# Adjacency as byte pairs in a two-layer graph attention kernel, with VectorE emptying the transposed banks and ScalarE comparing 104 of 128 units

## Chip, cores and metric

One core of a Trainium2 chip runs the whole program. The metric is the device time of one execution in microseconds (us); lower is better.

## What is computed

`x` is 4096 x 128 (f32), `adj` is 4096 x 4096 (int32, 0 or 1, about 1 in 500 is set, the diagonal always). Two layers of masked attention follow each other, each with a residual and a layer norm:

```python
# layer 0, four heads of 32
Wh = (h @ W).reshape(N, H, D)
e = s_src[:, None, :] + s_dst[None, :, :]
e = jnp.where(e >= 0, e, 0.2 * e)
e = jnp.where(adj[:, :, None] > 0, e, NEG_INF)
h_prime = einsum('ijh,jhd->ihd', softmax(e, axis=1), Wh);  elu
# layer 1, one head of 128, the same mask
x_tan = _logmap0(x);  e = leaky_relu(x_tan @ a[:D] + (x_tan @ a[D:]).T, 0.2)
x_tan_prime = softmax(where(adj > 0, e, NEG_INF), axis=1) @ x_tan
return _proj(_expmap0(x_tan_prime))
```

The exponential of a leaky sum splits into factors of i and of j on either side of zero. So for each pair (i, j) the kernel needs only two bits: is j a neighbour, and is s_i + d_j negative. The softmax becomes two mask products, one with the mask of all neighbours (or of those above zero) and one with the mask of those below, times weighted values held as three bf16 parts.

## The kernel before

**Chunks and units.** The first layer goes over 4 chunks (`NC`) of 1024 rows i. In a chunk there are 32 units `u`: head `h` (4) times group `g` of `JU` = 4 tiles of 128 columns j. A unit has a slot in `ring` (4 slots), each with two halves of 128 x 4096 bytes, "above" and "below".

**What a unit costs each engine.** Either ScalarE (`act_unit`, L741) or VectorE (`dve_compare`, L756) compares: four instructions of 128 x 1024, one per tile j, each reading f32 and writing one byte. The string "AVAVAAVA", repeated, says who: 20 units of 32 on ScalarE, 12 on VectorE. VectorE then ANDs the result with the masks (L777 after ScalarE, L781 after itself). For a unit that is not `DIRECT` it also XORs to get "above" (L786). `DIRECT` is "DD-D----" repeated, 12 of 32. TensorE (`pe_chunk`, L825) does 8 row tiles times 4 tiles j, two matmuls each: two of 99 columns for a unit that is not direct; one of 99 with `masks` and one of 198 with "below" for a direct one. Each loads 128 x 128 fp8 weights, a contiguous 128 bytes per partition.

**Masks.** GpSimd issues casting DMAs (`load_adj`, L399) that bring 128 rows of `adj` into one of two bf16 tiles. TensorE transposes 8 blocks of 128 x 128 at a time (`turn_group`, L413) into one of four banks. ScalarE empties the bank into `raw_masks` (`take_group`, L421). There are 32 such groups in a chunk (`QT` = 4 per tile). In the end VectorE turns `raw_masks` into `masks` with 8 instructions (`clean_masks`, L493). `masks` is one buffer. The groups for chunk c + 1 are turned between units 6 and 27 of chunk c; ScalarE takes them 3 units later. SyncE stores `masks` to DRAM for the second layer (`keep`, L854) and reloads rows of scores.

**Order.** Each engine runs its units in order. A compare of unit u waits until TensorE is done with unit u - 4. After the last unit of a head, VectorE reduces four banks (L795) and weighs them (L210 to L223), which frees the banks for TensorE. The steps that close a chunk (L688 to L714) lie between the first units of the next. Chunks 0 to 2 are in a loop with register counts.

**Start.** `x` is loaded in four parts; then tile 0 and tile 1 of the adjacency are loaded, and tile t once the tile t - 1 is turned and the queue comes to it. Between the 16 steps of the projection (L565), from step 8 on, TensorE turns one group per step, 8 in all. VectorE then finds bounds (L149 to L171), and prepares weighted values (`prepare_sides`, L460 to L469) with casts on ScalarE (`round_sides`, L481), between which ScalarE takes three groups at a time. Then VectorE cleans all masks of chunk 0 and the block of units starts (first compare at 91.65 us). GpSimd weighs one of the sides (L436) after its eight tile loads.

**Second layer.** 8 runs of 512 rows; `load_masks` (L1008) fetches the masks, ScalarE (L1250) and VectorE (L1350) compare half of the tiles each (512 elements), TensorE multiplies 387 columns at a time (L1283, the first run L1301).

```python
    ON_ACT = [who == "A" for who in H * "AVAVAAVA"]
    DIRECT = [how == "D" for how in H * "DD-D----"]
            act.activation(dst[:, j:j + GQ, t * P:(t + 1) * P],
                           turn_bank[q % 4][:, :].bitcast(BF16).rearrange("p (j i) -> p j i", i=P),
                           ACT.Relu, scale=2.0, saturate=False).then_inc(turned_out, 1)
            dve.tensor_scalar(masks[:, :].bitcast(I32)[:, here], raw_masks[:, :].bitcast(I32)[:, here], TWOS, SIGNS,
                              ALU.bitwise_and, ALU.bitwise_or).then_inc(mask_ready, 1)
```

Of the kernel before, what the change touches and what calls it, by code (L numbers as in the profile page):

```python
# [15 lines left out]
F32, BF16, FP8, I32, U8 = (mybir.dt.float32, mybir.dt.bfloat16, mybir.dt.float8e4, mybir.dt.int32, mybir.dt.uint8)  # L16
# [4 lines left out]
P = 128  # L21
# [8 lines left out]
TWOS = 0x40404040  # L30
SIGNS = 0x80808080 - (1 << 32)
# [21 lines left out]
def two_layer_gat(nc, x, adj, W, a0, a1, out):  # L53
# [3 lines left out]
    x_rows = x.rearrange("(t p) f -> p t f", p=P)  # L57
    out_rows = out.rearrange("(t p) f -> p t f", p=P)
# [12 lines left out]
    ON_ACT = [who == "A" for who in H * "AVAVAAVA"]  # L71
# [13 lines left out]
    LAG = 3  # L85
# [16 lines left out]
    masks_kept = nc.dram_tensor("masks_kept", (NC, P, T, C // 4), I32, kind="Internal").ap()  # L102

    ctx = ExitStack()
    with ctx:
# [120 lines left out]
        def general_attention(layer, heads, width, flag_ap, d_rows_dram, s_of, values_in, summed, finish):  # L226
# [3 lines left out]
            with local:  # L230
# [13 lines left out]
                B = N // BANK  # L244
                with nc.Block() as block:
                    @block.sync
                    def _(sp):
                        with sp.If(sp.value_load(flag_ap, min_val=0, max_val=1) > 0):
                            sp.dma_start(d_rows[:, :, :], d_rows_dram.rearrange("(o h) n -> o h n", o=1)
                                         .broadcast_to([P, heads, N])).then_inc(loaded, 16)  # L250
                            if values_in is None:
                                sp.dma_start(v[:, :, :], values_kept).then_inc(loaded, 16)
                            with sp.Fori(0, T) as it:
                                sp.wait_ge(adj_used, it + 1)
                                sp.dma_start(adj_tile[:, :], adj[bass.ds(it * P, P), :]).then_inc(adj_in, 16)

                    @block.vector
                    def _(dve):
                        with dve.If(dve.value_load(flag_ap, min_val=0, max_val=1) > 0):
                            dve.memset(rowwise[:, 3:4], 0.0).then_inc(adj_used, 1)  # L260
                            dve.wait_ge(loaded, 16 if values_in is not None else 32)
                            with dve.Fori(0, T) as it:
                                dve.wait_ge(adj_in, it * 16 + 16)
                                dve.tensor_scalar(keep[:, :], adj_tile[:, :], 0.0, None, ALU.is_gt).then_inc(chain, 1)
                                dve.tensor_scalar(away[:, :], adj_tile[:, :], 0.0, -NEG_INF, ALU.is_le, ALU.mult)\
                                    .then_inc(adj_used, 1)
                                for h in range(heads):
                                    q = it * heads + h
                                    c = it * (5 * heads + 1) + 5 * h + 1
                                    dve.wait_ge(chain, c)  # L270
                                    dve.tensor_scalar(e[:, :], d_rows[:, h, :], s_of(it, h), None, ALU.add).then_inc(chain, 1)
                                    dve.wait_ge(chain, c + 1)
                                    dve.scalar_tensor_tensor(out=e[:, :], in0=e[:, :], scalar=SLOPE, in1=e[:, :],
                                                             op0=ALU.mult, op1=ALU.max).then_inc(chain, 1)
                                    dve.wait_ge(chain, c + 2)
                                    dve.tensor_tensor(e[:, :], e[:, :], keep[:, :], ALU.mult).then_inc(chain, 1)
                                    dve.wait_ge(chain, c + 3)
                                    dve.wait_ge(adj_used, it + 2)
                                    dve.tensor_tensor(e[:, :], e[:, :], away[:, :], ALU.add).then_inc(chain, 1)
                                    dve.wait_ge(chain, c + 4)  # L280
                                    dve.reduce_max(rowwise[:, 0:1], e[:, :], axis=AXX).then_inc(chain, 1)
                                    dve.wait_ge(chain, c + 5)
                                    dve.tensor_scalar(rowwise[:, 1:2], rowwise[:, 0:1], -1.0, None, ALU.mult)\
                                        .then_inc(masked, 1)
                                    dve.wait_ge(expd, q + 1)
                                    dve.reciprocal(rowwise[:, 3:4], rowwise[:, 2:3]).then_inc(normed, 1)
                                    for n in range(B):
                                        dve.wait_ge(turned, q * B + (n + 1))
                                        dve.tensor_copy(eT[:, n % 2, :], bank[n % 2][:, :]).then_inc(turned_out, 1)
                                    dve.wait_ge(sums, q + 1)  # L290
                                    dve.wait_ge(normed, q + 1)
                                    dve.tensor_scalar(one(summed[:, bass.ds(it, 1), h * width:(h + 1) * width]),
                                                      bank[2][:, 0:width], rowwise[:, 3:4], None, ALU.mult)\
                                        .then_inc(given, 1)
# [64 lines left out]
        idle = masks[:, :].bitcast(F32)  # L359
# [26 lines left out]
        adj_in = sems("adj_in0", "adj_in1")  # L386
        a1_taken, turned, turned_out, mask_ready, kept, pool_done = sems(
            "a1_taken", "turned", "turned_out", "mask_ready", "kept", "pool_done")
# [8 lines left out]
        def load_adj(pool, b, t):  # L397

            pool.dma_start(adj_tiles[:, t % 2, :], adj[bass.ds(b * C + t * P, P), :]).then_inc(adj_in[t % 2], 16)  # L399

        def turn_group(pe, b, q):

            t = q // QT
            if q % QT == 0:
                pe.wait_ge(adj_in[t % 2], b * (8 * CT) + 16 * (t // 2 + 1))
            if isinstance(b, int) and b == 0 and q < 4:
                pass
            else:
                hold(pe, turned_out, b * Q + (q - 3))
            dst = turn_bank[q % 4][:, :].bitcast(BF16)  # L410
            for k in range(GQ):
                j = (q % QT) * GQ + k
                last = pe.transpose(dst[:, k * P:(k + 1) * P], adj_tiles[:, t % 2, j * P:(j + 1) * P], ident_b[:, :])  # L413
            last.then_inc(turned, 1)

        def take_group(act, b, q):

            t, j = q // QT, (q % QT) * GQ
            hold(act, turned, b * Q + (q + 1))
            dst = raw_masks[:, :].rearrange("p (j i) -> p j i", i=C)  # L420
            act.activation(dst[:, j:j + GQ, t * P:(t + 1) * P],  # L421
                           turn_bank[q % 4][:, :].bitcast(BF16).rearrange("p (j i) -> p j i", i=P),
                           ACT.Relu, scale=2.0, saturate=False).then_inc(turned_out, 1)
# [64 lines left out]
        def clean_masks(dve, b, g):  # L488

            if g == 0:  # L490
                dve.wait_ge(turned_out, b * Q + Q)
            here = slice(g * (JU * C // 4), (g + 1) * (JU * C // 4))
            dve.tensor_scalar(masks[:, :].bitcast(I32)[:, here], raw_masks[:, :].bitcast(I32)[:, here], TWOS, SIGNS,  # L493
                              ALU.bitwise_and, ALU.bitwise_or).then_inc(mask_ready, 1)

        with nc.Block() as block:
            @block.sync
            def _(sp):
# [3 lines left out]
                for k in range(XPARTS):  # L502
                    some = slice(k * T // XPARTS, (k + 1) * T // XPARTS)
                    sp.dma_start(feat[:, some, :], x_rows[:, some, :]).then_inc(x_in[k], 16)
# [13 lines left out]
            def _(pool):  # L518
# [98 lines left out]
            def _(dve):  # L617
# [46 lines left out]
                for g in range(UH):  # L664
                    clean_masks(dve, 0, g)

# [52 lines left out]

        def act_count(u):  # L720
# [9 lines left out]
        def act_unit(act, c, u):  # L730
# [18 lines left out]
        def dve_compare(dve, c, u):  # L749
# [10 lines left out]
        def dve_unit(dve, c, u, clean=False):  # L760
# [4 lines left out]
            if clean and g + 1 < UH:  # L765
                clean_masks(dve, c, g + 1)
# [3 lines left out]
            m = masks[:, :].bitcast(I32)[:, g * (JU * C // 4):(g + 1) * (JU * C // 4)]  # L770
            done = unit_ready if DIRECT[u] else below_ready
            if clean:
                dve.wait_ge(mask_ready, c * UH + (g + 1))
# [28 lines left out]
        def pe_chunk(pe, c, build):  # L802

            for u in range(U):
# [6 lines left out]
                for t in range(CT):  # L811
# [3 lines left out]
                    for k in range(JU):  # L815
                        j = g * JU + k
                        mine = slice(k * C + t * P, k * C + (t + 1) * P)
                        if DIRECT[u]:
                            of_all = masks[:, j * C + t * P:j * C + (t + 1) * P]
                            weighed = ((of_all, 0, PARTS * K0), (below[:, mine], 0, W0))  # L820
# [613 lines left out]
```

## Time and profile before

| | us |
|---|---|
| three executions | 1074.44, 1074.69, 1074.98 (median 1074.69) |
| the profiled execution, first to last instruction (span) | 1073.5 |
| start, to the first compare of chunk 0 | 91.65 |
| chunk 0, then 1, 2, 3, each to the first bank reduced of its last head | 134.9, 138.0, 137.5, 128.0 |
| from there to the end | 443.5 |
| busy: TensorE, VectorE, ScalarE, GpSimd | 901.4, 897.8, 608.6, 51.3 |

The page gives the profiled execution's span and no separate time of its own; the span is 1.2 us under the median of the three. Busy times of TensorE include modelled ends, so a matmul's price is read from the distance between starts and not from its duration. On VectorE successive instructions overlap a little, so there too start to start is used where it matters.

### The profile page before, as it was taken

The numbers are of one execution on the slowest core, as the hardware profiler recorded it, in microseconds if no ns is written. First come the engines' busy times: TensorE is split into PE (matmuls) and PEld (weight loads), VectorE is DVE, ScalarE is ACT, GpSimd is POOL, SyncE is SP. The second block draws the span as 40 slices with busy tenths as digits, with TensorE's granted clock in tenths as the row PEclk, the third lists the DMA queues.
The fourth block names the chain that finished last, engine by engine and source line by source line (L and its number), as shares of the span: only waits on it lengthen the run. The fifth ranks groups of instructions, "written<-read, shape, count | busy, mean of one in ns | idle before, by whom it ended". The sixth has DMA issues, their size and how long they took to land. (4 is left out here: it accounts for less than half of the span.)

```text
span 1073.5 us, 27634 instructions
## 1 busy us (share of the span) xinstructions
PE 901.4 (84%) x11508; PEld 744.5 (69%) x11508; DVE 897.8 (84%) x1648; ACT 608.6 (57%) x672; POOL 51.3 (5%) x59
## 2 busy tenths in 40 slices
PE   7644999987999889998888950388999999999990
PEld 6534999987999889998787950354555555555550
DVE  6956888989998999988999976989888788778825
ACT  3685899967899677996755711344414225134101
POOL 1030000000000000000000000800000000000000
PEclk9756999989999999999999985689999999999996
DMA  8865355615555245530210003301130321303000
GB/s 179 221 118 190 82 116 108 108 35 184 104 109 104 59 159 118 99 82 22 126 54 22 2 1 101 79 1 50 49 89 12 99 60 39 89 16 92 0 10 11
DMA packets 50686, 85.88 MB, mean 80 GB/s; under 512 B 1346, under 2 KB 42756, under 8 KB 45828
## 3 DMA queue, kind: packets, MB, share of 16 engines
q0 software_dynamic: 4608, 33.56, 17.1%
q1 hardware_dynamic: 41732, 48.47, 14.3%
q10 hardware_dynamic: 4224, 2.10, 0.7%
q8 instruction: 92, 1.51, 0.6%
q14 instruction: 30, 0.25, 0.1%
HBM read 96.54 MB, written 21.14 MB: 110 GB/s over the span
## 5 line engine op out<-in xcount | busy, mean ns | idle before, releaser
L825 PE MATMUL bank<-moving,ring 128*128 128x99 bf16 (+1 forms) x6656 | 455.7, 219 | 18.9 <-DVE ring L786 18.9
L825 PEld LDWEIGHTS bank<-moving,ring 128*128 128x128 fp8e4 x6656 | 390.9, 98 | 24.3 <-issue 11.5
L741 ACT ACTIVATE ring<-s_rows,scores 128x1024 fp8e4<-128x1024 f32 x320 | 340.5, 1141 | 107.9 <-PE bank L825 97.6
L1283 PE MATMUL bank<-moving,pair 128*128 128x387 bf16 x1792 | 299.9, 329 | 3.8 <-DVE evac L1372 3.8
L1283 PEld LDWEIGHTS bank<-moving,pair 128*128 128x128 fp8e4 x1792 | 175.6, 98 | 128.1 <-DVE evac L1372 4.2
L825 PE MATMUL bank<-moving,masks 128*128 128x99 bf16 x1536 | 211.8, 211 | 33.3 <-DVE evac L795 18.0
L825 PEld LDWEIGHTS bank<-moving,masks 128*128 128x128 fp8e4 x1536 | 152.5, 100 | 33.4 <-issue 24.7
L756 DVE TENSOR_SCALAR ring<-s_rows,neg_d 128x1024 uint8<-128x1024 f32 x192 | 131.5, 748 | 10.4 <-PE bank L825 6.6
L1210 ACT ACTIVATE small<-small 128x4 f32<-128x4 f32 x24 | 4.9, 205 | 219.1 <-DVE small L1156 180.3
L421 ACT ACTIVATE raw_masks<-bank 128x1024 fp8e4<-128x1024 bf16 x128 | 121.9, 1028 | 6.8 <-PE bank L413 5.2
L777 DVE SCALAR_TENSOR_TENSOR ring<-ring,masks 128x1024 int32<-128x1024 int32 x80 | 97.6, 1220 | 20.9 <-ACT ring L741 20.9
L413 PE MATMUL bank<-ident_b,adj_tiles 128*128 128x128 bf16 x1024 | 78.9, 232 | 26.7 <-ACT raw_masks L421 16.0
L786 DVE TENSOR_TENSOR ring<-masks,ring 128x1024 int32<-128x1024 int32 x80 | 98.0, 1225 | 2.7
L1250 ACT ACTIVATE pair<-s_rows,scores 128x512 fp8e4<-128x512 f32 x128 | 79.5, 708 | 20.7 <-DVE result L1190 16.2
L413 PEld LDWEIGHTS bank<-ident_b,adj_tiles 128*128 128x128 bf16 x1024 | 67.3, 104 | 31.3 <-ACT raw_masks L421 12.6
L1372 DVE TENSOR_REDUCE evac<-bank 128x129 f32<-128x387 f32 x64 | 31.6, 553 | 43.3 <-PE bank L1283 37.2
L1350 DVE TENSOR_SCALAR pair<-s_rows,neg_d 128x512 uint8<-128x512 f32 x128 | 58.6, 521 | 0.0
L781 DVE TENSOR_TENSOR ring<-ring,masks 128x1024 int32<-128x1024 int32 x48 | 58.5, 1218 | 0.0
L1301 PE MATMUL bank<-moving,pair 128*128 128x387 bf16 x256 | 44.3, 336 | 15.7 <-DVE pair L1362 15.7
L1301 PEld LDWEIGHTS bank<-moving,pair 128*128 128x128 fp8e4 x256 | 25.5, 100 | 34.4 <-issue 17.8
L1362 DVE TENSOR_TENSOR pair<-pair 128x1024 int32<-128x1024 int32 x32 | 39.2, 1225 | 1.1
L399 POOL DMA_DIRECT2D adj_tiles<-in_adj_dram x32 | 19.2, 601 | 433.9 <-PE bank L413 414.1
(218 smaller groups left out, 602.7 us busy)
## 6 DMA issues: line engine op xcount, KB each, us to landing
adj_tiles<-in_adj_dram POOLq DMA_DIRECT2D x32, 1024.0 KB, 8.4
masks_kept<-masks SPq DMA_DIRECT2D x4, 4096.0 KB, 13.0
pair<-masks_kept SPq DMA_DIRECT2D x8, 2048.0 KB, 9.8
s_rows<-score_rows SPq DMA_DIRECT2D x16, 512.0 KB, 3.6
feat<-in_x_dram SPq DMA_DIRECT2D x4, 512.0 KB, 6.1
values_kept<-masks SPq DMA_DIRECT2D x1, 2048.0 KB, 12.2
s_rows<-score_rows SPq DMA_DIRECT2D x8, 256.0 KB, 9.6
out_dram<-result ACTq DMA_DIRECT2D x8, 256.0 KB, 2.3
```

The source lines that it names most:

```text
L413: last = pe.transpose(dst[:, k * P:(k + 1) * P], adj_tiles[:, t % 2, j * P:(j + 1) * P], ident_b[:, :])
L421: act.activation(dst[:, j:j + GQ, t * P:(t + 1) * P], turn_bank[q % 4][:, :].bitcast(BF16).rearrange("p (j i) -> p j i", i=P), ACT.Relu, s ...
L741: last = act.activation(below[:, k * C:(k + 1) * C], s_rows[:, h % 2, :], ACT.Sign, bias=scores[:, j, h:h + 1], saturate=False)
L756: last = dve.tensor_scalar(below[:, k * C:(k + 1) * C], s_rows[:, h % 2, :], neg_d[:, h, j:j + 1], float(TWO), ALU.is_lt, ALU.mult)
L777: dve.scalar_tensor_tensor(out=below, in0=below, scalar=1, in1=m, op0=ALU.logical_shift_right, op1=ALU.bitwise_and).then_inc(done, 1)
L781: dve.tensor_tensor(below, below, m, ALU.bitwise_and).then_inc(done, 1)
L786: dve.tensor_tensor(above, m, below, ALU.bitwise_xor).then_inc(unit_ready, 1)
L825: last = pe.matmul(bank[b][:, at + lo:at + hi], mask, moving[:, j, h, lo:hi], start=first, stop=(j == T - 1), skip_group_check=True)
L1250: last = act.activation(pair[:, y, 1, j * R:(j + 1) * R], s_rows1[:, y, :], ACT.Sign, bias=scores1[:, j, 0:1], saturate=False)
L1283: last = pe.matmul(bank[2 * t + side][:, 0:PARTS * K1], pair[:, y, side, j * R + t * P:j * R + (t + 1) * P], moving1[:, j, side * PARTS * ...
L1301: last = pe.matmul(bank[2 * t + side][:, 0:PARTS * K1], pair[:, 0, side, j * R + t * P:j * R + (t + 1) * P], moving1[:, j, side * PARTS * ...
L1350: last = dve.tensor_scalar(below[:, j * R:(j + 1) * R].bitcast(U8), s, neg_d1[:, 0, j:j + 1], float(TWO), ALU.is_lt, ALU.mult)
```

## The change

Adjacency is cast to bytes and not to bf16, and two neighbouring bytes of a row are transposed as one bf16. So a tile has 16 transposes, not 32, and a chunk 16 groups (`QT` = 2), not 32. Rows and columns are numbered so that tile 2q + r holds the elements of parity r of 256. In `masks` and in both halves of a slot the bytes of tiles 2q and 2q + 1 alternate. Every compare therefore writes bytes at a step of 2, and every weight load of L825 and L1283 reads 128 bytes at a step of 2.

The bank is emptied by a multiply and an add on 16-bit integers straight into `masks`; `raw_masks` and `clean_masks` are gone, `masks` has two buffers, and `featT` and `values` lie in the second. In chunk 0 ScalarE still empties (16 groups); for chunks 1 to 3 VectorE does (16 each, after unit u it takes the groups of step u - 2). Four adjacency tiles are loaded ahead, not two. ScalarE compares 26 of 32 units, VectorE 6; 14 of 32 are direct. Loops over chunks are written out. The second layer's mask loads and the loads of `x` and stores of the result have runs twice as long.

```diff
-    ON_ACT = [who == "A" for who in H * "AVAVAAVA"]
+    ON_ACT = [who == "A" for who in H // 2 * ("AVAAAAVA" "AAVAAAAA")]
-    DIRECT = [how == "D" for how in H * "DD-D----"]
+    DIRECT = [how == "D" for how in H // 2 * ("DD-D----" "DD-D-D--")]
-    QT = T // GQ
+    QT = PAIRS // GQ
+    AHEAD = 4
-    LAG = 3
+    DVE_LAG = 2
-        masks = sb("masks", [P, T * C], FP8, fast0)
-        raw_masks = sb("raw_masks", [P, T * C], FP8, fast0)
+        masks = sb("masks", [P, 2, T * C], FP8, fast0)
-        adj_tiles = sb("adj_tiles", [P, 2, N], BF16, fast0)
+        adj_tiles = sb("adj_tiles", [P, AHEAD, N], U8, fast0)
-        idle = masks[:, :].bitcast(F32)
+        idle = masks[:, 1, :].bitcast(F32)
...
+        def take_group_dve(dve, b, q):
+            t, j = q // QT, (q % QT) * GQ
+            dve.wait_ge(turned, b * Q + (q + 1))
+            dst = masks[:, b % 2, :].bitcast(U16).rearrange("p (j i) -> p j i", i=C)
+            dve.tensor_scalar(dst[:, j:j + GQ, t * P:(t + 1) * P],
+                              turn_bank[q % 4][:, :].bitcast(U16).rearrange("p (j i) -> p j i", i=P),
+                              float(TWO), BOTH_SIGNS, ALU.mult, ALU.add).then_inc(turned_out, 1)
...
-                load_adj(pool, 0, 1)
-                for t in range(2, CT):
-                    pool.wait_ge(turned, (t - 1) * QT)
+                for t in range(1, AHEAD):
+                    load_adj(pool, 0, t)
+                for t in range(AHEAD, CT):
+                    pool.wait_ge(turned, (t - AHEAD + 1) * QT)
                     load_adj(pool, 0, t)
...
-                for g in range(UH):
-                    clean_masks(dve, 0, g)
...
+        def j_tile(half, k):
+            return half.rearrange("p (q i r) -> p q i r", i=C, r=2)[:, k // 2, :, k % 2]
-                last = act.activation(below[:, k * C:(k + 1) * C], s_rows[:, h % 2, :], ACT.Sign,
+                last = act.activation(j_tile(below, k), s_rows[:, h % 2, :], ACT.Sign,
...
-                last = dve.tensor_scalar(below[:, k * C:(k + 1) * C], s_rows[:, h % 2, :], neg_d[:, h, j:j + 1],
+                last = dve.tensor_scalar(j_tile(below, k), s_rows[:, h % 2, :], neg_d[:, h, j:j + 1],
...
+            if u == 0:
+                dve.wait_ge(turned_out, (c + 1) * Q)
...
                         for u in which:
-                            dve_unit(dve, c, u, clean)
+                            dve_unit(dve, c, u)
+                            if c + 1 < NC:
+                                for q in groups_at(u - DVE_LAG):
+                                    if q == 0 and c > 0:
+                                        dve.wait_ge(unit_done, SLOTS + c * U)
+                                        dve.wait_ge(kept, c * 16)
+                                    take_group_dve(dve, c + 1, q)
```

## Rows read from the trace of the kernel before

**Rows 1.** The page: busy time of each engine

```profile
PE 901.4 (84%) x11508; PEld 744.5 (69%) x11508; DVE 897.8 (84%) x1648; ACT 608.6 (57%) x672; POOL 51.3 (5%) x59
```

**Rows 2.** Busy time by chunk: window, length, PE, PEld, DVE, ACT, POOL, clock, DMA share

```profile
91.60:226.50 134.90, 125.51 (x2304) 124.58 (x2304) 115.58 (x146) 121.86 (x120) 6.18 (x10) 0.96 0.55 127
226.50:364.50 138.00, 126.24 (x2304) 124.22 (x2304) 128.69 (x182) 114.73 (x113) 5.07 (x8) 0.98 0.47 109
...
502.00:630.00 128.00, 112.21 (x2004) 110.06 (x2005) 121.47 (x173) 77.34 (x73) 0.00 (x0) 0.96 0.12 43
```

**Rows 3.** VectorE's groups in chunk 1: busy us, mean ns, idle before them

```profile
L756 DVE TENSOR_SCALAR ring<-s_rows,neg_d 128x1024 uint8<-128x1024 f32 x48 | 32.8, 747 | 2.1 <-PE bank L825 1.4 <-DVE attended L223 0.7
L786 DVE TENSOR_TENSOR ring<-masks,ring 128x1024 int32<-128x1024 int32 x20 | 24.5, 1225 | 0.7
L493 DVE TENSOR_SCALAR masks<-raw_masks 128x1024 int32<-128x1024 int32 x8 | 5.4, 686 | 0.1
```

**Rows 4.** Waits in chunk 1: us in total, times, longest

```profile
ACT ring L741 <- PE bank L825: 21.2, 8, 9.3
PE bank L825 <- DVE evac L795: 4.9, 2, 4.2
```

**Rows 5.** ScalarE's timeline: the four compares of a unit; eleven banks emptied

```profile
240.25 4.25 ACT L741 ACTIVATE ring<-s_rows,scores 128x1024 fp8e4<-128x1024 f32 x4
67.62 10.16 ACT L421 ACTIVATE raw_masks<-bank 128x1024 fp8e4<-128x1024 bf16 x11
```

**Rows 6.** TensorE's timeline at full clock: one group turned, one unit, direct pairs

```profile
324.80 0.61 PE L413 MATMUL bank<-ident_b,adj_tiles 128*128 128x128 bf16 x8
325.24 3.08 PE L825 MATMUL bank<-moving,ring 128*128 128x99 bf16 x64
333.11 0.25 PE L825 MATMUL bank<-moving,ring 128*128 128x198 bf16 x1
...
333.88 0.25 PE L825 MATMUL bank<-moving,ring 128*128 128x198 bf16 x1
```

**Rows 7.** Weight loads in chunk 1's lines: of fp8, and of bf16

```profile
L825 PEld LDWEIGHTS bank<-moving,ring 128*128 128x128 fp8e4 x1632 | 94.7, 97 | 6.6 <-issue 6.4
L413 PEld LDWEIGHTS bank<-ident_b,adj_tiles 128*128 128x128 bf16 x256 | 15.3, 97 | 1.8 <-issue 1.8
```

**Rows 8.** VectorE reading a bank: 128 and 396 elements

```profile
69.04 0.29 DVE L658 TENSOR_SCALAR mean_values<-bank 128x128 f32<-128x128 f32 x1
L795 DVE TENSOR_REDUCE evac<-bank 128x132 f32<-128x396 f32 x16 | 8.3, 561 | 0.5 <-PE bank L825 0.3
```

**Rows 9.** VectorE's and TensorE's timelines at the end of the start

```profile
85.17 4.91 DVE L493 TENSOR_SCALAR masks<-raw_masks 128x1024 int32<-128x1024 int32 x8 [15.58 <-ACT raw_masks L421]
91.65 2.79 DVE L756 TENSOR_SCALAR ring<-s_rows,neg_d 128x1024 uint8<-128x1024 f32 x4 [1.57 <-PEq L878]
97.54 0.24 PE L825 MATMUL bank<-moving,masks 128*128 128x99 bf16 x1 [14.06 <-DVE ring L777]
```

**Rows 10.** Timelines of GpSimd and TensorE in the start

```profile
10.06 0.72 POOL L399 DMA_DIRECT2D adj_tiles<-in_adj_dram  x1 [7.97 <-DMA feat<-in_x_dram]
11.75 0.53 POOL L399 DMA_DIRECT2D adj_tiles<-in_adj_dram  x1 [0.97 <-DMA feat<-in_x_dram]
72.38 1.92 POOL L436 TENSOR_TENSOR ring<-masks,below_d 128x1024 f32<-128x1024 f32 x1
26.33 0.61 PE L413 MATMUL bank<-ident_b,adj_tiles 128*128 128x128 bf16 x8
```

**Rows 11.** Landing of the loads issued at 10.06 and at 11.75 us

```profile
DMA to landing us min/median/max: 8.2/8.2/8.2
DMA to landing us min/median/max: 11.4/11.4/11.4
```

**Rows 12.** The chain of waits in the second layer: VectorE's compares, then TensorE

```profile
731.55 1.67 DVE pair L1350 x4
748.81 299.92 PE bank L1283 x1792
```

More of the change, by code:

```diff
@@ L56, in two_layer_gat, with paired, adj_rows @@
     T = N // P
-    x_rows = x.rearrange("(t p) f -> p t f", p=P)
-    out_rows = out.rearrange("(t p) f -> p t f", p=P)
+    PAIRS = N // (2 * P)
+    x_rows = x.rearrange("(q p r) f -> p q (r f)", p=P, r=2)
+    out_rows = out.rearrange("(q p r) f -> p q (r f)", p=P, r=2)
+    def paired(ap):
+        return ap.rearrange("p (q r) f -> p q (r f)", r=2)
+    def adj_rows(q, r):
+        some = bass.ds(q * 2 * P, 2 * P) if not isinstance(q, int) else slice(q * 2 * P, (q + 1) * 2 * P)
+        return adj[some, :].rearrange("(p r) n -> r p n", r=2)[r]
     CT = 8
@@ L252, in _ @@
                                 sp.dma_start(v[:, :, :], values_kept).then_inc(loaded, 16)
-                            with sp.Fori(0, T) as it:
-                                sp.wait_ge(adj_used, it + 1)
-                                sp.dma_start(adj_tile[:, :], adj[bass.ds(it * P, P), :]).then_inc(adj_in, 16)
+                            with sp.Fori(0, PAIRS) as iq:
+                                for r in range(2):
+                                    sp.wait_ge(adj_used, iq * 2 + (r + 1))
+                                    sp.dma_start(adj_tile[:, :], adj_rows(iq, r)).then_inc(adj_in, 16)
                     @block.vector
@@ L261, in _ @@
                             dve.wait_ge(loaded, 16 if values_in is not None else 32)
[L262 to L294, printed above, removed]
@@ L385, in two_layer_gat @@
             "mean_ready", "exp_asked", "exp_given", "scores_out", "values_out")
-        adj_in = sems("adj_in0", "adj_in1")
-        a1_taken, turned, turned_out, mask_ready, kept, pool_done = sems(
-            "a1_taken", "turned", "turned_out", "mask_ready", "kept", "pool_done")
+        adj_in = sems(*(f"adj_in{k}" for k in range(AHEAD)))
+        a1_taken, turned, turned_out, kept, pool_done = sems("a1_taken", "turned", "turned_out", "kept", "pool_done")
         s_in = sems("s_head_in0", "s_head_in1")
@@ L404, in turn_group @@
             if q % QT == 0:
[L405 to L409, printed above, removed]
+                pe.wait_ge(adj_in[t % AHEAD], 16 * (b * (CT // AHEAD) + t // AHEAD + 1))
+            if b > 0 or q >= 4:
+                pe.wait_ge(turned_out, b * Q + (q - 3))
             dst = turn_bank[q % 4][:, :].bitcast(BF16)
+            src = adj_tiles[:, t % AHEAD, :].bitcast(BF16)
             for k in range(GQ):
                 j = (q % QT) * GQ + k
-                last = pe.transpose(dst[:, k * P:(k + 1) * P], adj_tiles[:, t % 2, j * P:(j + 1) * P], ident_b[:, :])
+                last = pe.transpose(dst[:, k * P:(k + 1) * P], src[:, j * P:(j + 1) * P], ident_b[:, :])
             last.then_inc(turned, 1)
@@ L842, in _ @@
                 with only_if(pool, flag[0:1, 0:1], False):
-                    with pool.Fori(0, NC - 1) as c:
+                    for c in range(NC - 1):
                         for t in range(CT):
-                            pool.wait_ge(turned, c * Q + (Q + (t - 1) * QT))
+                            pool.wait_ge(turned, c * Q + (Q + (t - AHEAD + 1) * QT))
                             load_adj(pool, c + 1, t)
@@ L862, in load_s @@
                             .then_inc(s_in[h % 2], 16)
-                    with sp.Fori(0, NC - 1) as c:
+                    for c in range(NC - 1):
                         keep(c)
@@ L879, in _ @@
                     pe.sem_inc(acc_taken, NB)
-                    with pe.Fori(0, NC - 1) as c:
+                    for c in range(NC - 1):
                         pe_chunk(pe, c, True)
@@ L907, in _, with units @@
                 with only_if(dve, flag[0:1, 0:1], False):
-                    def units(c, which, clean=False):
+                    def units(c, which):
                         for u in which:
-                            dve_unit(dve, c, u, clean)
+                            dve_unit(dve, c, u)
[5 more added lines that the diff above has]
+                                    take_group_dve(dve, c + 1, q)
                             for h in range(H - 1):
@@ L918, in close @@
                         finish_ask(dve, attended[:, :, :], elu_asked)
-                    dve.wait_ge(mask_ready, UH)
                     units(0, range(DVE_ROT))
-                    with dve.Fori(0, NC - 1) as c:
+                    for c in range(NC - 1):
                         units(c, range(DVE_ROT, U))
-                        hold(dve, kept, c * 16 + 16)
-                        dve.wait_ge(unit_ready, c * U + U)
-                        clean_masks(dve, c + 1, 0)
                         for u in range(DVE_ROT):
-                            units(c + 1, (u,), u < UH)
+                            units(c + 1, (u,))
                             if u == CLOSE_AT:
@@ L1211, in close_act @@
             act.wait_ge(result_ready, e + 1)
-            act.dma_start(out_rows[:, run_rows(e), :], result[:, y, :, :]).then_inc(stored[y], 16)
+            pairs = bass.ds(e * (RT // 2), RT // 2) if not isinstance(e, int) else slice(e * RT // 2, (e + 1) * RT // 2)
+            act.dma_start(out_rows[:, pairs, :], paired(result[:, y, :, :])).then_inc(stored[y], 16)
         with nc.Block() as block:
```

123 lines of the change are left out of this document (76 added, 47 removed).

## The prediction, made before the change was run

> **What bounds the kernel now.** I read the page first. TensorE and VectorE are both busy for 84% of the span [rows 1], which settles nothing, so I cut the span into stages and asked in each which wait ends last.
>
> The start lasts 91.65 us. VectorE has finished its preparing at 69.6 us, stands idle for 15.58 us until ScalarE has emptied the last bank of turned adjacency, and then cleans all masks of chunk 0, 4.91 us; 1.6 us after that the units begin [rows 9]. So the emptying and the cleaning bound the start.
>
> In chunk 1 VectorE is busy 128.7 of 138.0 us, ScalarE 114.7 [rows 2]. Chunk 2 reads the same. TensorE's own need I work out from starts: a unit that isn't direct has 64 matmuls 45.7 ns apart, (3.08 - 0.21) / 63, so 2.92 us; a direct pair takes 128.3 ns, 0.77 us for six, so 4.11 us for the unit's 32; a transpose takes 56 ns, (0.61 - 0.216) / 7, the single durations being 0.21 and 0.216 us [rows 6]. 12 x 4.11 + 20 x 2.92 + 256 x 0.056 = 122.1 us. VectorE bounds chunks 1 to 3, with 9.3 us of gaps and waits in chunk 1. In chunk 0, without the closing steps, VectorE is busy only 115.6 us and TensorE is the heaviest with 122.1; the chunk takes 134.9. Of the 12.8 us above TensorE's need, 5.9 pass before its first matmul [rows 9] and about 3 are lost while its first unit runs at the lower clock. That leaves 4 us as the price of three nearly equal engines sharing four slots.
>
> In the second layer TensorE's matmuls run through for 299.9 us [rows 12]; nothing there is removed.
>
> **The change, part by part.**
>
> *Start.* 16 groups fewer for ScalarE are 16 x 0.92 = 15 us (10.16 us for eleven) [rows 5], and the cleaning goes. If nothing else were late, the units would begin at 69.6 + 1.6 = 71.2 us, 20.4 us sooner. But something is late next: the eight groups turned between the projection's steps now need tiles 0 to 3, where before they needed 0 and 1. Tile 0 lands at 10.06 + 8.2 = 18.3 us and tile 1 at 11.75 + 11.4 = 23.15, 4.9 us behind it in one queue [rows 10, 11]. At that pace tile 3 lands at 32.9 us, and the turn that waits for it stood at 26.33 us [rows 10]. Everything behind it in TensorE's order (the rest of the projection, then bounds and preparing) moves by 6.5 us. Units begin at 77.7: **-14**. The ends: -20.4 with no delay; if each tile took the whole 8.2 us, tile 3 lands at 42.9 and it is -4. GpSimd's weighing, at 72.4 us behind its eight issues [rows 10], follows tile 3's turn in place of tile 7's and comes sooner. The same holds for its later loads: their waits fall earlier.
>
> *VectorE in a chunk.* 24 compares go: 32.8 x 24/48 = 16.4 us. 8 cleans go: 5.4. Two XORs go: 2 x 1.22 = 2.5 [rows 3]. For six units the AND changes its form and not its price. What comes is 16 banks emptied, 128 x 1024 from a bank of 16-bit integers; no row has this. From below: the clean is the same operation on the same number of elements, 0.686 us [rows 3]. From above: bank reads of f32 take 0.29 us for 128 elements and 0.56 for 396 [rows 8], 1.01 ns an element, so 1.20 us. I take 0.67, as the clean is nearest in operation and size; +10.8 us, at most +19. Chunk 1's busy time becomes 128.7 - 24.3 + 10.8 = 115.2 us.
>
> The Trainium skill (VectorE: DVE Perf Modes, What auto-detection actually checks) says that two elements a cycle from a bank need every operand to be 16-bit at a step of 1, which holds here and not for the rows of f32. By its cycle table (120 + 512 cycles at 0.96 GHz) the estimate is 0.66 us, which would leave the sum as it is.
>
> *ScalarE.* 26 units x 4.27 = 111 us and 1 for the exponential, from 85.4 + 30 + 1 before [rows 5]: 112, unchanged in sum for chunks 1 and 2. The work is shifted from banks, which waited for nothing urgent, to compares, which TensorE waits for. The runs of six such units (25.6 us against 21 us of matmuls) have to be covered by its lead; it waited 21.2 us for slots in chunk 1 [rows 4], so there is some.
>
> *TensorE.* 14 x 4.11 + 18 x 2.92 + 128 x 0.056 = 117.3 us, 4.8 less; in chunk 3, without turns, 110.1, 2.3 more. Byte steps of 2 I take at nothing in all three engines: fp8 loads of 128 contiguous bytes and bf16 loads over 256 bytes both take 97 ns [rows 7], so the span of bytes isn't what a load costs.
>
> *New waits.* After unit u VectorE waits for the turn of step u - 2, with its next unit behind it, and TensorE behind that. TensorE does that turn before unit u - 2, and the next compare waits for unit u - 3 anyway; nothing. TensorE's turn needs the group four back, taken about three units ago; nothing. At unit 0 VectorE waits for groups it has emptied itself. SyncE's store of masks waits for the same count, with score rows behind it, and has more time than now. Written-out loops cost fetches of code beside a DMA share of 0.47 [rows 2]; nothing. In the second layer longer runs make loads shorter that are hidden.
>
> *Sum.* TensorE is now the heaviest, with VectorE at 115 and ScalarE at 112. Chunk 0: 117.3 plus the same 12.8, some 131: -4. Chunk 1: 117.3 plus 4 for sharing slots plus 4.9 for the banks of the last head, which it waits for now too [rows 4], 126.5: -11.5. Chunk 2: -11. Chunk 3: ScalarE 112 is the heaviest, VectorE 121.5 - 16.4 - 3.4 (five cleans) - 2.5 = 99; with 8 us of waits 120: -8. Together -14 - 4 - 11.5 - 11 - 8 = **-48.5 us** on a span of 1073.5, which stands 1.2 us under the median. Against the median it gives 1026 us.
>
> **Rivals.**
>
> *A, banks at one element a ns.* 8 us more on VectorE: 123 + 9.3 in chunks 1 and 2, so -5.5 and -5; the others stand. -36.5, 1038 us. For it: every bank read in the trace [rows 8].
>
> *B, compares to bytes at a step of 2 fall to one element a cycle.* 1.2 for 0.683 us, 24 of them: +12.4 a chunk. Chunk 1 is then 127.6 + 9.3 = 137. -14 - 3 - 1 - 0.5 - 7, and in the second layer's first two runs, where VectorE is on the chain, 32 compares of 0.39 us [rows 12] would take 0.61: +7. -18.5, 1056 us. Against it: the compare already writes single bytes at the fast rate.
>
> *C, the other side: weight loads at a step of 2.* Place: the 45.7 ns between the matmuls of 99 columns, which leave a load no room. All that the trace proves is that a load fits into the 56 ns of a transpose [rows 6]. At 56, 10.3 ns more on 18 x 64 loads and 10.7 on 14 x 32 pairs are 16.7 us a chunk: chunk 0 134 + 13.7, 1 and 2 134 + 9.3, 3 126.8 + 8; +12.8 + 5.3 + 5.8 + 6.8 - 14 = +16.7, 1091 us. It decides above some 53 ns, where 12 us a chunk eat the 48.5. The second layer's 387 columns cover it. Against it: the 97 ns of both kinds [rows 7].
>
> The Trainium skill (TensorE: Matmul & The Clock Gate, Weight-path perf modes) keeps the fast load at any column step up to 1,024, which is against C; but it also says that it reads 32 bits at a time, four fp8 or two bf16, and at a step of 2 only two fp8 lie in 32 bits, which is for C. No row here has such a load.
>
> *D, the work shifted onto ScalarE doesn't come off.* The runs of six use up the lead, ScalarE keeps its 21 us of waits for slots, and a chunk takes 112 + 21 = 133: -2 - 5 - 5 - 0, and the start -14. -26, 1049 us.
>
> **How the numbers follow.** Forecast 0.45, A 0.13, B 0.09, C 0.15, D 0.18. The forecast's own range is 1014 (start -20, 1.5 us less waiting a chunk) to 1036. The range 1014 to 1062 leaves out C and the tails. About 0.2% is what a measurement of this kernel can tell from no change. All but C are faster by more; C between 45.7 and 56 ns crosses zero, and I keep a little for mishaps: faster 0.81, same 0.03, slower 0.16.
>
> **What would show it.** First compare of chunk 0 at 77 to 78 us; the cleans (L493) gone; the new bank reads at 0.65 to 0.7 us; compares still 0.75 mean on VectorE and 1.14 on ScalarE; 64 matmuls in 3.1 us; chunk lengths 131, 126.5, 126.5, 120. Matmul starts over 46 ns apart in a run that waits for nothing would make it wrong at once, as would VectorE idling mostly for ScalarE at L777.

## The result, and the profile after

The changed kernel takes 1046.1 us, the median of four executions (1043.8 to 1047.8), against 1074.6 before (also four, one more than in the section above): a ratio of 0.9735, 95% interval 0.9721 to 0.9749. It is 28.5 us faster; 48.5 had been forecast. The profiled execution took 1046.3 us with a span of 1044.2; all stage times here and below are those of the profiled executions.

The stages are cut as before: at the first compare of chunk 0, then at the first bank reduced of each chunk's last head. First the four chunks (window, length, then busy us of PE, PEld, DVE, ACT, POOL, clock, DMA share, GB/s), to be held against [rows 2]:

```profile
84.07:218.54 134.47, 123.20 (x2165) 121.97 (x2165) 105.28 (x133) 115.91 (x111) 7.77 (x12) 0.93 0.66 110
218.54:348.00 129.46, 120.32 (x2181) 119.00 (x2178) 115.29 (x165) 110.57 (x107) 4.90 (x8) 0.99 0.49 84
348.00:477.45 129.45, 120.32 (x2181) 119.01 (x2179) 115.28 (x165) 110.58 (x107) 2.49 (x4) 0.99 0.31 66
477.45:601.13 123.68, 113.22 (x2021) 111.73 (x2019) 100.97 (x143) 103.94 (x100) 0.00 (x0) 0.97 0.08 30
```

| stage | before | after | change | forecast |
|---|---|---|---|---|
| start | 91.65 | 84.07 | -7.6 | -14 |
| chunk 0 | 134.8 | 134.5 | -0.4 | -4 |
| chunk 1 | 138.0 | 129.5 | -8.6 | -11.5 |
| chunk 2 | 137.5 | 129.45 | -8.1 | -11 |
| chunk 3 | 128.0 | 123.7 | -4.3 | -8 |
| to the end of the span | 443.5 | 443.1 | -0.4 | 0 |

VectorE is busy 115.3 us in chunk 1; the sum of the prediction said 115.2. So the prices of VectorE's work were right, and what is missing is idle time. The waits of chunk 1 (us in total, times, longest), against [rows 4]:

```profile
ACT ring L766 <- PE bank L849: 14.6, 7, 4.2
DVE ring L800 <- ACT ring L766: 9.7, 7, 2.3
...
PE bank L849 <- DVE evac L818: 4.9, 2, 2.7
...
PE bank L849 <- DVE ring L809: 3.6, 3, 2.0
```

Nobody is free of waits now: ScalarE waits for TensorE's slots, VectorE at its AND for ScalarE, TensorE for VectorE. Before, VectorE's waits for ScalarE in chunk 1 were 3.5 us. In chunk 0 they are the longest of all, 27.0 us against 12.6 before:

```profile
DVE ring L800 <- ACT ring L766: 27.0, 18, 3.3
```

Two rows of the groups by shape answer the unknown prices. The bank emptied by VectorE, and the compare that writes bytes at a step of 2:

```profile
L451 DVE TENSOR_SCALAR masks<-bank 128x1024 uint16<-128x1024 uint16 x48 | 32.8, 682 | 0.0
L781 DVE TENSOR_SCALAR ring<-s_rows,neg_d 128x1024 uint8<-128x1024 f32 x96 | 65.7, 750 | 3.3 <-PE bank L849 1.6 <-PEq L902 1.6
```

And TensorE's timeline, one unit that isn't direct, every weight load at a step of 2, against [rows 6]:

```profile
243.76 3.06 PE L849 MATMUL bank<-moving,ring 128*128 128x99 bf16 x64 [0.87 <-DVE ring L809]
```

(3.06 - 0.20) / 63 = 45.4 ns between matmuls, against 45.7. In the start the projection was held up by the tiles, as forecast. The turn that waits for tile 3, which stood at 26.33 us [rows 10]:

```profile
32.32 0.62 PE L434 MATMUL bank<-ident_b,adj_tiles 128*128 128x128 bf16 x8 [1.12 <-DMA adj_tiles<-in_adj_dram]
```

It was forecast for 32.9. That it came so close is partly luck: the first tile landed sooner than before (its turn began at 16.80 us), and by the turns that wait for them the tiles followed each other at 4.9, 5.8 and 4.8 us, where 4.9 each had been put. But VectorE's preparing, which took 28.9 us before (40.7 to 69.6), took 35.9 (46.5 to 82.5). Its timeline in that stretch, and GpSimd's:

```profile
46.52 1.23 DVE L490 TENSOR_TENSOR ring<-masks,above_d 128x1024 f32<-128x1024 f32 x1 [0.38 <-ACT above_d L635]
47.66 1.90 DVE L492 COPY ring<-above_d 128x32 f32<-128x32 f32 x1
49.47 1.21 DVE L490 TENSOR_TENSOR ring<-masks,above_d 128x1024 f32<-128x1024 f32 x1
...
53.96 5.28 DVE L499 TENSOR_TENSOR moving<-ring,moving 128x1056 bf16<-128x1056 f32 x2
59.16 3.13 DVE L490 TENSOR_TENSOR ring<-masks,above_d 128x1024 f32<-128x1024 f32 x1
62.21 0.18 DVE L492 COPY ring<-above_d 128x32 f32<-128x32 f32 x1
62.29 1.21 DVE L490 TENSOR_TENSOR ring<-masks,above_d 128x1024 f32<-128x1024 f32 x1
```

```profile
46.77 2.75 POOL L466 TENSOR_TENSOR ring<-masks,below_d 128x1024 f32<-128x1024 f32 x1 [12.04 <-ACT below_d L636]
49.58 1.20 POOL L468 COPY ring<-below_d 128x32 f32<-128x32 f32 x1
50.85 2.09 POOL L201 CAST moving<-ring 128x1056 bf16<-128x1056 f32 x1
53.02 3.00 POOL L202 TENSOR_TENSOR ring<-ring,moving 128x1056 f32<-128x1056 f32 x1
56.08 2.06 POOL L203 CAST moving<-ring 128x1056 bf16<-128x1056 f32 x1
58.22 2.98 POOL L204 TENSOR_TENSOR moving<-ring,moving 128x1056 bf16<-128x1056 f32 x1
```

The same multiply takes 3.13 us while GpSimd works and 1.21 us right after; GpSimd's own took 1.92 us alone [rows 10] and 2.75 now.

Laid side by side, the two timelines read as turns, and not as a general slowing. GpSimd's multiply begins at 46.77 us under VectorE's, which keeps its 1.23 us; it ends at 49.52, its own 1.9 us after VectorE's has made way at 47.66. The copy that VectorE begins at 47.66 takes 0.19 us alone and ends at 49.56, with GpSimd's multiply. So it goes on up to VectorE's multiply of 59.16, which ends 1.1 us after GpSimd's last instruction (61.20).

### The profile page after: what moved, and what is told of

Its sections match the earlier page's. It is cut to its first block and busy times, and to the rows that moved or that the text cites. A ratio compares the mean times of both kernels' runs of the same rounds, so it can differ in the third digit from the quotient of the medians.

```text
span 1044.2 us, 25201 instructions
## 1 busy us (share of the span) xinstructions
PE 875.2 (84%) x10996; PEld 720.4 (69%) x10996; DVE 842.0 (81%) x1560; ACT 607.0 (58%) x656; POOL 57.2 (5%) x59
## 5 line engine op out<-in xcount | busy, mean ns | idle before, releaser
L766 ACT ACTIVATE ring<-s_rows,scores 128x1024 fp8e4<-128x1024 f32 x416 | 438.5, 1139 | 74.5 <-PE bank L849 57.8
L849 PE MATMUL bank<-moving,masks 128*128 128x99 bf16 x1792 | 247.7, 211 | 42.9 <-DVE evac L818 21.5
L849 PEld LDWEIGHTS bank<-moving,masks 128*128 128x128 fp8e4 x1792 | 178.3, 100 | 44.8 <-DVE ring L800 26.6
L800 DVE SCALAR_TENSOR_TENSOR ring<-ring,masks 128x1024 int32<-128x1024 int32 x104 | 126.9, 1221 | 63.0 <-ACT ring L766 62.8
L809 DVE TENSOR_TENSOR ring<-masks,ring 128x1024 int32<-128x1024 int32 x72 | 88.2, 1225 | 2.5
L781 DVE TENSOR_SCALAR ring<-s_rows,neg_d 128x1024 uint8<-128x1024 f32 x96 | 65.7, 750 | 3.3 <-PE bank L849 1.6
L434 PE MATMUL bank<-ident_b,adj_tiles 128*128 128x128 bf16 x512 | 40.8, 227 | 22.6 <-ACT masks L442 14.8
L1327 PEld LDWEIGHTS bank<-moving,pair 128*128 128x128 fp8e4 x256 | 25.7, 100 | 35.9 <-issue 19.5
L434 PEld LDWEIGHTS bank<-ident_b,adj_tiles 128*128 128x128 bf16 x512 | 33.2, 102 | 25.0 <-ACT masks L442 9.3
L818 DVE TENSOR_REDUCE evac<-bank 128x132 f32<-128x396 f32 x64 | 32.1, 558 | 2.9 <-PE bank L849 2.5
L451 DVE TENSOR_SCALAR masks<-bank 128x1024 uint16<-128x1024 uint16 x48 | 32.8, 682 | 0.0
```

What stands on the lines that cost most here:

```text
L434: last = pe.transpose(dst[:, k * P:(k + 1) * P], src[:, j * P:(j + 1) * P], ident_b[:, :])
L451: dve.tensor_scalar(dst[:, j:j + GQ, t * P:(t + 1) * P], turn_bank[q % 4][:, :].bitcast(U16).rearrange("p (j i) -> p j i", i=P), float(TWO ...
L766: last = act.activation(j_tile(below, k), s_rows[:, h % 2, :], ACT.Sign, bias=scores[:, j, h:h + 1], saturate=False)
L781: last = dve.tensor_scalar(j_tile(below, k), s_rows[:, h % 2, :], neg_d[:, h, j:j + 1], float(TWO), ALU.is_lt, ALU.mult)
L800: dve.scalar_tensor_tensor(out=below, in0=below, scalar=1, in1=m, op0=ALU.logical_shift_right, op1=ALU.bitwise_and).then_inc(done, 1)
L809: dve.tensor_tensor(above, m, below, ALU.bitwise_xor).then_inc(unit_ready, 1)
```

## The experiments

Two questions were open: what lengthened the preparing, and what fills a chunk beyond TensorE's 117.3 us. In the expectations P and T are theories of the first, R and S of the second. All edits are to the changed kernel. A kernel with a ratio had four executions. The others had one, so their whole times are good to some 2 us.

### GpSimd's weighing put behind VectorE's

```diff
                 pool.wait_ge(exp_given, 2)
+                pool.wait_ge(side_done, len(sides0))
```

> The changed kernel, but GpSimd begins its weighing of one side only when VectorE has finished its seven. Theory P (the two engines weigh at once and slow each other): VectorE's preparing, 46.5 to 82.5 us in the changed kernel, shrinks from 35.9 us to the 28.9 us it took before the change, GpSimd's own six instructions from 14.4 to about 9 us; units then wait for GpSimd, so their first compare comes at 75.5 + 9 + 1.6 = about 86 us, two later than now. Rival T (adjacency and value loads in flight slow the preparing): it stays at 35 to 36 us, and the first compare comes at 93 us.

Measured: preparing from 46.4 to 75.2 us, 28.8 us; first compare at 86.07; 1046.0 us in all. The same instructions of VectorE and of GpSimd, now apart:

```profile
51.37 2.53 DVE L499 TENSOR_TENSOR moving<-ring,moving 128x1056 bf16<-128x1056 f32 x2
53.81 1.22 DVE L490 TENSOR_TENSOR ring<-masks,above_d 128x1024 f32<-128x1024 f32 x1
```

```profile
74.81 1.91 POOL L466 TENSOR_TENSOR ring<-masks,below_d 128x1024 f32<-128x1024 f32 x1 [40.22 <-DVE moving L499]
...
81.63 2.11 POOL L204 TENSOR_TENSOR moving<-ring,moving 128x1056 bf16<-128x1056 f32 x1
```

P holds to a tenth of a microsecond, and T falls: loads were in flight here too (DMA share 0.47 from 46 to 76 us, against 0.38 from 46 to 82 in the changed kernel). The Trainium skill (GPSIMD Engine Reference, Specifications) says that the two engines share their SBUF interfaces and contend where VectorE reads two SBUF inputs or runs in a two-port mode. The multiplies are of the first kind, and 7 us is what all of it costs here; the copies of 32 elements have one input, and no run tells by which case they wait.

### No weighing on GpSimd

```diff
-    ON_POOL = 1
+    ON_POOL = 0
```

> The changed kernel, with all eight sides weighed by VectorE and none by GpSimd. Theory P: preparing takes four pairs of 7.3 us, 29.2 us, so the first compare of a unit comes at 46.5 + 29.5 + 1.6 = about 78 us, 6 us sooner than in the changed kernel, and the whole takes about 1040 us. Rival T: each pair stays slow where loads are in flight, the first pairs keep their 12.6 us, the preparing takes 36 us plus half a pair, and the first compare comes at 86 us or later.

Measured: first compare at 78.30 us, 5.8 sooner; 1042.0 us, ratio to the kernel before 0.9683 (0.9659 to 0.9707). The start kept its gain; chunks 0 and 1 gave 2.4 us of it back (135.4 and 130.9), with a lower mean clock in both (0.92 and 0.97).

### Four groups turned within the projection

```diff
-            return range(n - 8, n - 7) if n >= 8 else range(0)
+            return range(n - 12, n - 11) if n >= 12 else range(0)
-            left = list(range(T // 2 - 8, Q))
+            left = list(range(T // 2 - 12, Q))
-                for q in range(T // 2 - 8, Q):
+                for q in range(T // 2 - 12, Q):
```

> The changed kernel, but only four groups of adjacency (tiles 0 and 1) are turned between the last four steps of the projection; tiles 2 and 3 follow with the others. Theory: the 5.8 us by which the projection ended later (34.06 for 28.25 us) come from its waiting for tiles 2 and 3, so it ends at 28 to 29 us again, and preparing starts at about 41 us. ScalarE has 12 groups left for its gaps, three after each pair, which fits. First compare at 78 to 79 us if GpSimd's weighing still collides. Rival: ScalarE's additional groups push its casts back and half of the gain is lost, first compare at 81 us.

Measured: preparing starts at 38.7 us and lasts 36.0, GpSimd still beside it; first compare at 77.08, 7.0 sooner; 1038.2 us. The whole delay was the wait for tiles 2 and 3, and a little more than the delay came back.

### Two tiles ahead

```diff
-    AHEAD = 4
+    AHEAD = 2
```

> The changed kernel with two adjacency tiles loaded ahead and not four. Chunks 1 to 3 as in the changed kernel within 0.3 us (129.5, 129.5, 123.7), since a tile is needed later than it lands by far. In the start tile 2 is issued once tile 0 is turned, at 18 us, while tile 1 is still landing (21.7 us), so the queue hardly runs dry: the projection ends at 34 to 36 us in place of 34.1, and the first compare comes at 84 to 86 us. If depth was what mattered and not the number of tiles needed, the projection would end at 40 us.

Measured: the projection ends at 36.4 us, the first compare comes at 86.61, chunks 131.9, 129.45, 129.4, 123.7; 1046.8 us. The four-deep load is worth 1 to 2.5 us in the start (with two tiles ahead the projection ended at 36.4 us here and at 35.1 in the kernel with five slots below, against 34.1) and nothing later. It was the number of tiles needed early that cost time.

### VectorE's units spread evenly

```diff
-    ON_ACT = [who == "A" for who in H // 2 * ("AVAAAAVA" "AAVAAAAA")]
+    ON_ACT = [u not in (1, 6, 11, 17, 22, 27) for u in range(U)]
```

> The changed kernel, with VectorE's six units of a chunk at 1, 6, 11, 17, 22, 27 in place of 1, 6, 10, 17, 22, 26: the runs of ScalarE's units are 4, 4, 5, 4, 4, 5 in place of 4, 3, 6, 4, 3, 6. Work is the same on all engines. Theory R (the runs of six use up ScalarE's lead): chunks 0 to 3 take 131, 126.5, 126.5, 121 us in place of 134.5, 129.5, 129.4, 123.7; VectorE's waits for ScalarE at its AND in chunk 1 fall from 9.7 us to under 5. Rival S (three engines with nearly equal work share four slots, and VectorE's 5 us at the end of each head open the gap): no chunk changes by more than 1 us, and the waits stay at 8 to 11 us.

Measured: chunks 131.2, 127.0, 128.2, 120.4; 1038.4 us, ratio 0.9662 (0.9645 to 0.9678). VectorE's waits for ScalarE in chunk 1 fell from 9.7 only to 7.5 us, in chunk 2 to 9.0. The time moved as R said (except chunk 2, 1.3 in place of 3 us), the waits did not fall as it said. So the runs of six cost 1.3 to 3.3 us in each of chunks 1 to 3, and most of the waiting is something else. Chunk 0 doesn't count here: kernels with the old runs took 131.9 us too (see below). And the profiled execution was the fastest of its four, 3.4 us under their median.

### Two more units on VectorE

```diff
-    ON_ACT = [who == "A" for who in H // 2 * ("AVAAAAVA" "AAVAAAAA")]
+    ON_ACT = [who == "A" for who in H * "AVAAAAVA"]
```

> The changed kernel, with VectorE comparing 8 units of a chunk (AVAAAAVA repeated) and ScalarE 24. ScalarE's need falls from 111 to 102.5 us, VectorE's busy time in chunk 1 rises from 115.3 to 120.7. Theory R (VectorE's idle time at its AND is ScalarE coming late in long runs): that idle time falls from 9.7 to under 3 us and chunk 1 takes 127 to 128 us in place of 129.5, chunk 3 121 in place of 123.7. Rival S (nearly equal loads on shared slots cost the same waits wherever the work lies): chunk 1 takes 120.7 + 14 = 134 to 135 us.

Measured: chunks 126.0, 127.9, 127.9, 119.35; 1030.8 us. VectorE works 5 us more a chunk and the chunk gets shorter. Its waits for ScalarE in chunk 1 are down to 2.8 us, and ScalarE waits the more:

```profile
ACT ring L766 <- PE bank L849: 24.7, 11, 4.3
...
DVE ring L800 <- ACT ring L766: 2.8, 2, 2.0
```

S as it was put (the same waits wherever the work lies) falls. 26 units were too many for ScalarE with four slots; with 24 it is early again.

### The shares of before

```diff
-    ON_ACT = [who == "A" for who in H // 2 * ("AVAAAAVA" "AAVAAAAA")]
+    ON_ACT = [who == "A" for who in H * "AVAVAAVA"]
-    DIRECT = [how == "D" for how in H // 2 * ("DD-D----" "DD-D-D--")]
+    DIRECT = [how == "D" for how in H * "DD-D----"]
```

> The changed kernel with the shares of before: ScalarE compares 20 units of a chunk and VectorE 12, and 12 are direct; VectorE still empties the banks. It separates the shift of compares from the rest. VectorE's busy time in chunk 1 becomes 115.3 + 16.4 + 2.4 = 134 us, and it waits for nobody: chunk 1 takes 134 + 6 = 140 us, 2 us more than the kernel before (16 emptied banks of 0.6 us for 8 cleans of 0.6). Chunk 3, where nothing is emptied, takes 125 us, 3 less than before. The whole is then 1074.6 - 7.6 + 2 + 2 - 3 = about 1068 us. Rival: if ScalarE's freedom from the banks were itself worth something, chunk 1 would stay under 138.

Measured: 1050.7 us, 17 better than expected; chunks 129.0, 134.7, 134.6, 124.2. Chunk 1 stayed under 138 us, as the rival said. Chunk 1 by engine:

```profile
214.01:348.71 134.70, 121.66 (x2176) 119.43 (x2176) 132.71 (x191) 86.01 (x82) 4.99 (x8) 0.96 0.47 80
```

VectorE is busy 132.7 of 134.7 us. Before it was busy 128.7 of 138.0 [rows 2]. So with the same shares, the rest of the change (banks on VectorE, half as many of them, two mask buffers, written-out loops) adds 4 us to VectorE's work and takes 7.3 us from its idle time. Against this kernel the shift of compares and the two direct units bring 5.2 and 5.1 us in chunks 1 and 2, 0.5 in chunk 3, and lose 5.5 in chunk 0 (2.9 against the kernels of the same shares that took 131.9 us there). The whole times differ by 4.6 us of the 28.5. Chunk 1 repeats to 0.1 us in the changed kernel and the three others that leave the units alone and run at the same mean clock.

### A fifth slot

```diff
-    SLOTS = 4
+    SLOTS = 5
-    AHEAD = 4
+    AHEAD = 2
-            below = slot_halves(u)[1]
+            below = slot_halves(c * U + u)[1]
```

(and so wherever a slot is named, since 32 is no multiple of 5).

> The changed kernel with five slots in the ring in place of four; for the room it loads two adjacency tiles ahead and not four (the next kernel has that alone). With a fifth slot ScalarE may run a unit further ahead, so its 14.6 us of waits for TensorE and VectorE's 9.7 us for ScalarE in chunk 1 should both shrink if four slots are what couples the engines: chunk 1 at 124 to 126 us, VectorE's waits at its AND under 5 us. If the work of the heaviest engine plus the emptied banks at head ends sets the chunk, it stays within 1 us of 129.5.

Measured: chunks 124.6, 122.7, 122.7, 116.0; 1016.9 us, 30 less than with two tiles ahead alone, and chunk 1 is shorter than the 124 to 126 us expected. Chunk 1 by engine, and its waits:

```profile
210.12:332.81 122.69, 118.51 (x2181) 117.55 (x2178) 114.92 (x164) 110.43 (x106) 4.88 (x8) 1.00 0.51 87
```

```profile
ACT ring L766 <- PE bank L849: 11.5, 6, 3.0
...
PE bank L849 <- DVE evac L818: 2.6, 2, 2.3
DVE ring L800 <- ACT ring L766: 1.6, 1, 1.6
```

The work is the same to 0.4 us on VectorE and ScalarE. VectorE's wait for ScalarE went from 9.7 to 1.6 us. So four slots coupled the engines, and at 122.7 us the chunk stands 5.4 above TensorE's need.

### All together

Five slots, two tiles ahead, nothing on GpSimd, four groups in the projection:

> Five slots and two tiles ahead, no weighing on GpSimd, four groups between the projection's steps. If the three causes found so far are separate, they add: first compare at 28.3 + 10.5 + 29.9 + 1.6 = about 71 us (84.1 in the changed kernel; 72 to 73 if the later tiles are late for ScalarE's gaps), then chunks of 124.6, 122.7, 122.7, 116.0 and 443 to the end: a span of 1000, 1002 us in all, 7% under the kernel before. If the earlier start only moves the loads of the next chunk onto the units, chunk 0 gives back some us and it stays at 1006 or more.

Measured: first compare at 72.51 us, chunks 124.6, 122.7, 122.7, 116.0, then 442.6; 1005.1 us, ratio 0.9366 (0.9347 to 0.9385). The causes add to within 1.2 us in the profiled span (1001.2 for 1000) and 3 us in the median (1005.1 for 1002). Then with VectorE's units spread:

> The same with VectorE's six units at 1, 6, 11, 17, 22, 27. If the longer lead of a fifth slot already covers the runs of six, this changes no chunk by more than 0.7 us; if runs still matter, chunks 1 and 2 fall from 122.7 to 121 us, where TensorE's own 117.3 leaves little more to take.

Measured: 70.86 us, chunks 125.5, 121.7, 121.7, 115.0; **999.9 us**, ratio 0.9315 (0.9299 to 0.9330). Chunks 1 to 3 fell by 1.1, 1.1 and 1.0 us and chunk 0 grew by 0.8, between the two expectations. Chunks 0 to 3 together give 2.4 us; the rest between the two profiled executions lies in the start (1.65) and behind the chunks (1.6), which the edit does not explain. Last with eight units:

> The same with VectorE comparing 8 units of a chunk. With four slots this took chunk 1 from 129.5 to 127.9 us. With five slots VectorE's idle time is already down to some 7 us in chunk 1, its busy time would be 120.3, so the chunk should take 123 to 125 us, no better than 122.7; chunk 0, where VectorE has no closing steps, 122 to 124.

Measured: 71.01 us, chunks 124.1, 124.4, 124.35, 116.55; 1004.8 us. Chunks 1 and 2 take 1.6 us more than with six units, where the same edit saved 1.5 us with four slots; the whole is no different. With five slots the shift of two units is no longer worth making.

## Why the prediction was right or wrong

**The direction and the range** held: 1046.1 lies between 1014 and 1062. The likeliest value, 1026, was 20 us too low, and the measured time lay outside the forecast's own range, which ended at 1036.

**Prices.** A bank on VectorE was put at 0.67 us and took 0.68, so rival A falls. The estimate of 0.66 us for 16-bit operands that the prediction worked out from the Trainium skill (VectorE: DVE Perf Modes, its cycle table) agrees to 0.02; the f32 rows [rows 8] did not carry over. Compares at a step of 2 kept 0.75 us, so B falls. Weight loads at a step of 2 leave 45.4 ns between matmuls, so C falls. Of the two things that the Trainium skill says (TensorE: Matmul & The Clock Gate, Weight-path perf modes), the one on column steps agrees: a load at a step of 2 still takes 97 ns in chunk 1. The one on 32 bits does not show in the time.

**The start** was -14 and came to -7.6. The step on the tiles held: the projection ended 5.8 us later, 6.5 had been said. The step that failed is "GpSimd's weighing ... comes sooner", which stood at nothing. It comes to lie on VectorE's preparing, and that costs 7.0 us; the first experiment shows it by moving one wait. Before, the queue of tile loads had kept the two apart by chance. (That queue is misread in two places: the program issues tile t once tile t - 2 is turned, not t - 1, so the weighing stood behind tile 5's turn and not tile 7's.)

**The chunks** were -34.5 and came to -21.4. VectorE's 115.2 and TensorE's 117.3 us stand. The term that failed is "4 for sharing slots". I had read it off chunk 0 of the kernel before, where ScalarE compared 20 units. With 26 units in runs of up to six it was 12.2 us in chunk 1 (129.5 - 117.3) with the 4.9 of the banks in it, so 7 and not 4. The fifth slot brings the 12.2 down to 5.4. Rival D had a part of the mechanism, the runs of six, and too large a price: it let ScalarE keep 21 us of waits and came to 133 us for chunk 1; its waits shrank to 14.6. Two slips in the sums change nothing: 117.3 + 12.8 is 130 and not 131, and D's 133 us would have made chunk 3 longer by 5, where 0 was put.

**The weighing of the parts** was wrong behind a sum that half cancelled. I held that ScalarE's banks "waited for nothing urgent" and that the shift of compares carried the gain. The kernel with the old shares shows that most of the gain comes without the shift: its chunks are 3 to 6 us shorter than before, and the shift adds 4.6 us to the whole. That the gain comes of ScalarE's freedom from the banks is argued and not shown. Of VectorE's 9.3 idle us in chunk 1 before, the trace puts only 3.5 to waits for ScalarE's compares and 0.5 to another of its results; 1.7 were waits for TensorE.

**Chunk 0** fell 3.6 us short, and its 17.2 us above TensorE's 117.3 can be taken apart in the changed kernel's trace. 5.65 pass before the first matmul (89.72). TensorE then ran 6.0 us at the lower of the two granted clocks, 1.2 GHz, up to 95.7; direct pairs start 0.25 us apart there and 0.13 later, so half of it, 3.0 us, is lost. These two terms were in the forecast. Not in it were TensorE's waits for VectorE's reduced banks at the ends of two heads, 5.3 us (4.9 had been put into chunk 1 alone), and two further stretches at the lower clock, 123.0 to 126.4 and 187.9 to 191.3, each beginning within such a wait and each costing 1.5 us. In all that is 17 us; the 4 of sharing took this shape here.

```profile
PE bank L849 <- DVE evac L818: 5.3, 2, 2.7
```

Part of this is not the program's. Five kernels have the same units in chunk 0. The late-weighing one has the same wait of 2.66 us at the first head end, and its clock did not fall there; its clock also rose 3.4 us after the first matmul and not 6.0. By half of 2.6 and half of 3.0 us its chunk 0 should be 2.8 us shorter, and it was 2.6 shorter. Of the five, three took 131.9, 131.9 and 132.4 us at a mean clock of 0.95 (late weighing, two tiles ahead, four groups), the changed kernel 134.5 at 0.93, the one without weighing on GpSimd 135.4 at 0.92. Why the clock differs between executions is open.

**Left open.** What took away VectorE's idle time of the kernel before wasn't taken apart: who empties the banks, fewer groups, the second mask buffer and written-out loops all changed together. Five slots in the kernel before, with its two large mask buffers, weren't tried.

## What to carry to other kernels

When three engines pass a ring of buffers around with loads within a few per cent of each other, the ring's depth can decide how much of a balanced share is realised: here one more slot was worth 30 us, more than the whole change, and it shifted which share was best. A sum of busy times tells which engine is heaviest and not how much is lost in passing; take that loss from a kernel with the new shares, or keep a wide range for it. And work that comes free to start earlier must be priced where it now lands: GpSimd beside VectorE cost VectorE 7 us that it had not cost 25 us later.

## What was unexpected of the hardware

VectorE and GpSimd hold each other up, and the traces read as if they took turns, instruction by instruction. VectorE's multiply of two SBUF tensors, 128 x 1024, took up to 3.13 us for 1.22, and a copy of 32 elements 1.90 for 0.19; GpSimd's six instructions took 14.4 us for 9.0. Work laid beside work gained little: with GpSimd's 9.0 us beside VectorE's and not behind, the first compare came only 2.0 us sooner (84.07 against 86.07).

The granted clock rose 3.4 us after TensorE's first matmul of the units in one execution and 6.0 us after it in another, and 3.4 us at the lower level began within a wait of 2.66 us in one and not in the other; together this moves chunk 0 by 2.6 us, of the order of the spread of whole executions of the changed kernel, 1043.8 to 1047.8.
